# Splitting key loads, reading a flag later and moving a scaling to GpSimd in a four-layer attention kernel

## The reference, cut to what matters

```
x = x + tanh(g_xattn[l]) * cross_attention_l(layernorm(x), ctx, mask_l)
x = x + tanh(g_ffn[l])   * feed_forward_l(layernorm(x))
```

```
attn = softmax(q @ k.T * scale + mask);  out = attn @ v
```

```
topk_scores, idx = top_k(scores, 32);  w = softmax(topk_scores);  out = w @ v[idx]
```

```
l2norm(t) = t / maximum(norm(t), 1e-12)
q = l2norm(q) * q_scale;  k = l2norm(k) * k_scale
q, k = rotary(q), rotary(k)         # local attention over windows of 32
```

## Time and profile before

| what | value |
|---|---|
| median of 3 runs | 8553.93 us (8548.58 to 8557.4) |
| the profiled execution, its own time | 8551.03 us |
| its span in the trace | 8549.2 us |
| mean granted TensorE clock | 0.816 of full |
| VectorE busy | 6960.8 us (81%) |
| TensorE busy | 5875.3 us (69%) |
| ScalarE busy | 4913.9 us (57%) |
| GpSimd busy | 669.4 us (8%) |

### The profile page before, as it was taken

One profiled execution on the slowest core, in us unless ns is written; L12 is line 12 of the kernel. 1 busy time (PEld: TensorE's weight loads), 2 busy tenths in 40 slices (PEclk: granted clock), 3 DMA queues, 4 the chain that ended last, 5 costly groups with the idle time before them and its releaser, 6 DMA issues. The chain is left out here.

```text
span 8549.2 us, 101651 instructions
## 1 busy us (share of the span) xinstructions
PE 5875.3 (69%) x35301; PEld 1769.4 (21%) x35301; DVE 6960.8 (81%) x14058; ACT 4913.9 (57%) x5921; POOL 669.4 (8%) x345
## 2 busy tenths in 40 slices
PE   5588887478888444533554777767788774788887
PEld 1011112111111111100110111144444441111113
DVE  5899991599995699999997999966766675999953
ACT  3177775057778344433444999944444550577782
POOL 1000000000000000000000000043433440000000
PEclk8599998689999555555556999978888885899998
DMA  7100001300000100000002000000000002000001
GB/s 217 28 2 16 16 1 36 77 3 15 16 2 1 24 8 8 8 8 8 8 4 47 16 16 3 1 28 13 13 9 13 11 4 55 3 15 16 2 1 45
DMA packets 111753, 174.94 MB, mean 20 GB/s; under 512 B 14665, under 2 KB 94357, under 8 KB 106254
## 3 DMA queue, kind: packets, MB, share of 16 engines
q1 hardware_dynamic: 111278, 168.91, 7.8%
HBM read 125.66 MB, written 43.21 MB: 20 GB/s over the span
## 5 line engine op out<-in xcount | busy, mean ns | idle before, releaser
L1008 DVE TENSOR_REDUCE a_partial<-a_row 128x1 f32<-128x494 f32 x4992 | 3021.5, 664 | 215.1 <-PE a_row L888 146.2
L974 ACT ACTIVATE a_prob<-a_score 128x1024 f32<-128x1024 f32 x2448 | 2360.5, 1021 | 606.5 <-PE a_score L901 606.2
L888 PE MATMUL a_row<-a_kg,a_qn 54*128 54x494 bf16 x4992 | 1027.8, 409 | 762.7 <-DVE a_partial L1008 660.9
L516 ACT COPY m_rows<-m_score 128x1536 f32<-128x1536 f32 (+1 forms) x640 | 760.9, 1250 | 919.3 <-PE m_score L495 804.1
L913 PE MATMUL a_acc<-a_prob,a_v_all 128*9 128x512 f32 x9792 | 1282.5, 596 | 1.7 <-ACT a_prob L974 1.4
L573 DVE MAX8 m_cand<-m_rows 128x8 f32<-128x192 f32 x4352 | 1220.7, 343 | 13.6 <-ACT m_rows L516 13.2
L495 PE MATMUL m_score<-m_kb,m_qb 54*128 54x512 bf16 (+1 forms) x1664 | 765.9, 608 | 309.4 <-ACT m_rows L516 243.8
L782 DVE SCALAR_TENSOR_TENSOR a_prob<-a_score,a_prob 128x1024 f32<-128x1024 f32 x816 | 924.6, 1211 | 50.3 <-ACT a_prob L758 50.3
L758 ACT ACTIVATE a_prob<-a_score,a_lower 128x1024 f32<-128x1024 f32 x816 | 865.4, 1110 | 72.9 <-PE a_score L701 21.2
L901 PE MATMUL a_score<-a_qb,a_kg 54*128 54x512 bf16 x4896 | 761.1, 379 | 34.7 <-ACT a_prob L974 20.8
L888 PEld LDWEIGHTS a_row<-a_kg,a_qn 54*128 54x128 bf16 x4992 | 241.9, 94 | 2357.4 <-DVE a_partial L1008 2232.4
(11 more groups left out here) (305 smaller groups left out, 5859.1 us busy)
## 6 DMA issues: line engine op xcount, KB each, us to landing
a_kg<-kst SPq DMA_DIRECT2D x64, 306.0 KB
kst<-kv_parts SPq DMA_DIRECT2D x48, 384.0 KB, 3.9
a_v_all<-vst SPq DMA_DIRECT2D x4, 3672.0 KB, 40.7
vst<-kv_va SPq DMA_DIRECT2D x48, 288.0 KB, 4.1
a_kg<-kst SPq DMA_DIRECT2D x64, 204.0 KB
e_cb<-comb SPq DMA_DIRECT2D x25, 512.0 KB
a_kg<-kst SPq DMA_DIRECT2D x64, 102.0 KB
qst<-q_parts SPq DMA_DIRECT2D x24, 256.0 KB, 3.2
```

The source lines that it names most:

```text
L516: act.copy(rows[i][:, c * CH:c * CH + n], score[(i * NCH + c) % 2][:, 0:n]).then_inc(copied, 1)
L888: pe.matmul(row[(use + half) % 3][:, 0:CW], qn[u % 2][rows, pair, i * P:(i + 1) * P], kg[u // NQC % 2][rows, pair, c * CW:(c + 1) * CW], s ...
L974: act.activation(prob[tile % PROBS][:, pair, :, :], score[use % 2][:, :, :], ACT.Exp).then_inc(slot_out, 1)
L1008: dve.tensor_reduce(partial[:, u % 2, 2 * item + half, c:c + 1], row[use % 3][:, 0:CW], AX, ALU.max).then_inc(reduced, 1)
```

## The change

Three edits, in four functions.

1. Key loads. In `attend_with_max` the semaphore of a group's keys becomes two, one for heads 0 and 1 and one for heads 2 and 3; TensorE waits for the first before fill 0 of a unit and for the second before fill 104. In `attend_to_top` the first group's keys are loaded in two column ranges, 768 columns (6 tiles) of all four heads first, then 6 tiles of the values, then the other 5760 columns and the other 45 tiles of the values; TensorE waits for the first parts at tile 0 and for the others at tile 6. That stage has 16 more key transfers and one more of the values.
2. `row_threshold`. `decide` is cut in two. `read_flags` (wait for the count, L552's copy) runs after tile 1 of the next, odd unit, and the rest (register, branch, columns kept, buffers freed) after its tile 8.
3. `local_transformer`. GpSimd scales the keys too, so every step has one `add_halves` and one `scale`. VectorE writes the reciprocal beside a constant 1e12 (a new tile `bounded`, set once by GpSimd) and takes the smaller of the two with a TENSOR_REDUCE.

```diff
-def load_key_rows(sp, dst, kst_h, kmask_l, sem):
+def load_key_rows(sp, dst, kst_h, kmask_l, sem, columns=slice(0, KPAD)):
...
-                     kst_h.rearrange("(d s) c -> d s c", s=PARTS)[:, 0:n, :]).then_inc(sem, 16)
+                     kst_h.rearrange("(d s) c -> d s c", s=PARTS)[:, 0:n, columns]).then_inc(sem, 16)
...
# row_threshold
+    READ_AT, DECIDE_AT = 1, 8
...
-            def decide(pair, slot):
-
+            def read_flags(pair):
                 dve.wait_ge(counted, pair + 2)
                 dve.tensor_copy(taken[:, :], flags[:, :]).then_inc(decided, 1)
+
+            def decide(pair, slot):
+
                 dve.wait_ge(decided, pair + 1)
...
                     last = dve.max(cand[i % 2][:, s, :], rows[i % 4][:, s * W:(s + 1) * W])
+                    if unit >= 3 and unit % 2 and s == READ_AT:
+                        read_flags((unit - 3) // 2)
+                    if unit >= 3 and unit % 2 and s == DECIDE_AT:
+                        decide((unit - 3) // 2, (unit - 3) % 4)
...
-                if i % 2 == 0 and pair is not None:
-                    decide(pair, (i - 2) % 4)
...
# attend_to_top
+    FIRST = 6
...
-            load_keys(0)
-            sp.dma_start(v_all[:, :, :, :], vst_l).then_inc(v_loaded, 16)
+            load_keys(0, kg_first, slice(0, FIRST * P))
+            sp.dma_start(v_all[:, 0:FIRST, :, :], vst_l[:, 0:FIRST, :, :]).then_inc(v_first, 16)
+            load_keys(0, kg_loaded[0], slice(FIRST * P, KPAD))
+            sp.dma_start(v_all[:, FIRST:KT, :, :], vst_l[:, FIRST:KT, :, :]).then_inc(v_loaded, 16)
...
+                    if u:
+                        pe.wait_ge(kg_loaded[u // NQC % 2], G * KEY_LOADS * (u // NQC // 2 + 1))
+                    else:
+                        pe.wait_ge(kg_first, G * KEY_LOADS)
+                if n == 2 * FIRST:
+                    pe.wait_ge(kg_loaded[0], G * KEY_LOADS)
...
                 if tile == 0:
+                    pe.wait_ge(v_first, 16)
+                if tile == FIRST:
                     pe.wait_ge(v_loaded, 16)
...
# attend_with_max
-                        pe.wait_ge(kg_loaded[u // NQC % 2], G * KEY_LOADS * (u // NQC // 2 + 1))
+                        pe.wait_ge(kg_loaded[u // NQC % 2][0], 2 * KEY_LOADS * (u // NQC // 2 + 1))
+                    if n % FILLS == FILLS // 2:
+                        u = n // FILLS
+                        pe.wait_ge(kg_loaded[u // NQC % 2][1], 2 * KEY_LOADS * (u // NQC // 2 + 1))
...
# local_transformer
+            pool.memset(bounded[:, :, :, :], 1.0 / NORM_FLOOR).then_inc(S["cleared"], 1)
...
-            def scale_queries(n):
-                pool.wait_ge(S["rn_q"], n // 2 + 1)
+            def scale(n):
+                pool.wait_ge(S["rn_ready"], n + 1)
...
-                    if s and (s - 1) % 2 == 0:
-                        scale_queries(n - 1)
+                    if s:
+                        scale(n - 1)
...
-            def invert(n, which):
+            def invert(n):
                 dve.wait_ge(S["root"], n + 1)
                 if n >= 2:
-                    dve.wait_ge(S[("scaled_q", "scaled_k")[which]], n // 2)
-                dve.reciprocal(rnorm[:, n % 2, :, :], norm[:, n % 2, :, :]).then_inc(S["inverted"], 1)
+                    dve.wait_ge(S["scaled"], n - 1)
+                dve.reciprocal(bounded[:, n % 2, :, 0:1], norm[:, n % 2, :, :]).then_inc(S["inverted"], 1)
                 dve.wait_ge(S["inverted"], n + 1)
-                if which == 0:
-                    dve.tensor_scalar(rnorm[:, 0, :, :], rnorm[:, 0, :, :], 1.0 / NORM_FLOOR, None,
-                                      ALU.min).then_inc(S["rn_q"], 1)
-                else:
-                    dve.wait_ge(S["added"], n + 1)
-                    dve.scalar_tensor_tensor(out=t1[n % T1S][:, :, :],
-                                             in0=rnorm[:, n % 2, :, :].to_broadcast([P, LH, LD]),
-                                             scalar=1.0 / NORM_FLOOR, in1=t1[n % T1S][:, :, :], op0=ALU.min,
-                                             op1=ALU.mult).then_inc(S["scaled_k"], 1)
+                dve.tensor_reduce(rnorm[:, n % 2, :, 0], bounded[:, n % 2, :, :], AX, ALU.min).then_inc(S["rn_ready"], 1)
```

More of the change, by code:

```diff
@@ L136, in load_key_rows @@
         sp.dma_start(dst[row:row + n * HD, :],
-                     kst_h.rearrange("(d s) c -> d s c", s=PARTS)[:, 0:n, :]).then_inc(sem, 16)
+                     kst_h.rearrange("(d s) c -> d s c", s=PARTS)[:, 0:n, columns]).then_inc(sem, 16)
         row += n * HD
-    sp.dma_start(dst[AUX:ROWS, :], kmask_l).then_inc(sem, 16)
+    sp.dma_start(dst[AUX:ROWS, :], kmask_l[:, columns]).then_inc(sem, 16)
 KEY_LOADS = 16 * (len(PRODUCTS) + 1)
@@ L591, in _ @@
             raise_flag(UNITS - 1, 3, UNITS // 2 - 1)
+            read_flags(UNITS // 2 - 1)
             decide(UNITS // 2 - 1, 2)
@@ L658, in attend_to_top @@
         kg_loaded, qb_loaded = ([m.sem(f"{n}_loaded{i}") for i in range(2)] for n in ("kg", "qb"))
-        cleared, v_loaded = m.sem("cleared"), m.sem("v_loaded")
+        cleared, kg_first, v_first, v_loaded = m.sem("cleared"), m.sem("kg_first"), m.sem("v_first"), m.sem("v_loaded")
         scored, exped, kept, summed = m.sem("scored"), m.sem("exped"), m.sem("kept"), m.sem("summed")
@@ L666, in _, with load_keys @@
         def _(sp):
-            def load_keys(g):
+            def load_keys(g, loaded, columns=slice(0, KPAD)):
                 for j in range(G):
-                    load_key_rows(sp, kg[g % 2][64 * (j % 2):64 * (j % 2) + ROWS, j // 2, :], kst_l[g * G + j], kmask_l,
-                                  kg_loaded[g % 2])
+                    load_key_rows(sp, kg[g % 2][64 * (j % 2):64 * (j % 2) + ROWS, j // 2, columns], kst_l[g * G + j], kmask_l,
+                                  loaded, columns)
             def load_queries(u):
@@ L678, in _ @@
             load_queries(0)
-            load_keys(0)
-            sp.dma_start(v_all[:, :, :, :], vst_l).then_inc(v_loaded, 16)
+            load_keys(0, kg_first, slice(0, FIRST * P))
+            sp.dma_start(v_all[:, 0:FIRST, :, :], vst_l[:, 0:FIRST, :, :]).then_inc(v_first, 16)
+            load_keys(0, kg_loaded[0], slice(FIRST * P, KPAD))
+            sp.dma_start(v_all[:, FIRST:KT, :, :], vst_l[:, FIRST:KT, :, :]).then_inc(v_loaded, 16)
             load_queries(1)
-            load_keys(1)
+            load_keys(1, kg_loaded[1])
             for u in range(UNITS - 2):
@@ L686, in _ @@
                 if u % NQC == 1 and u // NQC + 2 < NG:
-                    load_keys(u // NQC + 2)
+                    load_keys(u // NQC + 2, kg_loaded[u // NQC % 2])
         @block.tensor
@@ L816, in attend_with_max @@
         row = [m.ps(f"row{i}", [P, QC]) for i in range(3)]
-        kg_loaded, qn_loaded = ([m.sem(f"{n}_loaded{i}") for i in range(2)] for n in ("kg", "qn"))
+        qn_loaded = [m.sem(f"qn_loaded{i}") for i in range(2)]
+        kg_loaded = [[m.sem(f"kg_loaded{i}{pair}") for pair in range(2)] for i in range(2)]
         cleared, v_loaded = m.sem("cleared"), m.sem("v_loaded")
@@ L849, in load_keys @@
                     load_key_rows(sp, kg[g % 2][64 * (j % 2):64 * (j % 2) + ROWS, j // 2, :], kst_l[g * G + j], kmask_l,
-                                  kg_loaded[g % 2])
+                                  kg_loaded[g % 2][j // 2])
             def load_queries(u):
@@ L1564, in local_transformer @@
         norm, rnorm = m.sb("norm", [P, 2, LH, 1]), m.sb("rnorm", [P, 2, LH, 1])
+        bounded = m.sb("bounded", [P, 2, LH, 2])
         ssq = m.sb("ssq", [P, 2, LH])
@@ L1573, in local_transformer @@
             "cleared", "setup", "loaded", "wqk", "wvo", "w12", "tables", "shifted",
-            "proj", "squared", "roped", "added", "summed_sq", "root", "inverted", "rn_q", "scaled_q", "scaled_k", "turned_qk", "kept_qk",
+            "proj", "squared", "roped", "added", "summed_sq", "root", "inverted", "rn_ready", "scaled", "turned_qk", "kept_qk",
             "v_done", "v_kept", "sc_done", "maxed", "exped", "rs_ready", "rinv_ready", "normed", "turned", "pt_ready",
@@ L1627, in turn_heads @@
                 n = layer * STEPS + s
-                pe.wait_ge(S[("scaled_q", "scaled_k")[s % 2]], n // 2 + 1)
+                pe.wait_ge(S["scaled"], n + 1)
                 if s:
@@ L1934, in keep @@
                                     S["o_ready"], 1)
-            dve.wait_ge(S["cleared"], 3)
+            dve.wait_ge(S["cleared"], 4)
             dve.wait_ge(S["loaded"], 16 * 7)
@@ L1948, in _ @@
                     if s:
-                        invert(n - 1, (s - 1) % 2)
+                        invert(n - 1)
                 for t in range(LT + 2):
```

3 lines of the change are left out of this document (1 added, 2 removed).

## The result

The changed kernel takes 8318.35 us (median of 4 runs, 8317.42 to 8321.43), the kernel before 8552.7 us (4 runs, 8548.58 to 8557.4): ratio 0.9726, 95% interval 0.971 to 0.9743. That is 234.4 us faster. The spans of the two profiled executions, 8549.2 and 8315.6 us, differ by 233.6 us, and that can be split by stage, from the same event in both timelines to the next.

The account below looks back on a forecast made before the run. VectorE was taken to set the pace in layer 2's search and the local transformer, with key waits at stage starts. 46 + 8 + 60 + 81 - 0.6 = 194 us off 8551.0 gave 8360 us on the median's basis, range 8325 to 8432.

Parts of the forecast that it names:

- Keys by head pair: Three stages with a maximum: first fill comes 15.5 us earlier in each, 46 us in all (ends 12 and 52).
- a further head costs 8.1 us: Key loads: each head beyond the first adds 8.1 us from issue to fill, so two heads take 18.7 us.
- Rival C: Key loads: first pair's keys share bandwidth with transfers queued behind, 12 us gained instead of 46, time 8394; chance 0.07.
- Keys by columns: Layer 2's attention to the top: sums of tile 6 start earlier, 8 us gained (ends -4 and 14); values late next.
- Flags: Layer 2's search: decision hidden behind VectorE's queued work, 0.95 us in each of 63, 60 us (ends 0 and 66).
- rival A: Search: register load and branch drain VectorE's queue, decision stays in the open, 60 us less gained, 8420; chance 0.17.
- GpSimd: Local transformer: scaling keys on GpSimd shortens the step from 5.31 us, 81 us in six layers (ends 39 and 93).
- 4.35 a step with gaps: Local transformer's first phase: GpSimd's addition and scaling, 4.24 us of work, set a step of 4.35 us including gaps.
- before and behind them the path is as now: Local transformer: only the 14 steps between first and last scaling gain; the rest of each layer gains nothing.
- The reduce: Local transformer: the 128 x 16 reduce replacing VectorE's bounding instructions takes 0.25 us, making VectorE's step 3.97 us.
- Rival B: Local transformer: TensorE at 1.2 GHz sets the step, 5.31 us or more, that edit gives 0, 8441; chance 0.10.
- Rival D: Local transformer: VectorE and GpSimd exclude each other throughout, step 8.2 us, slower at 8683; chance 0.03.

Follow-up runs that it names:

- pairs alone: The kernel before with only the waits by head pair added in the three stages with a maximum: 8506.18 us (10 runs), ratio 0.9952.

## Why the prediction was right, and where it was not

Two terms of the sum failed, both too small: 60 us for the flags, where 76.6 were measured, and 81 us for the scaling, where it was 100.9. Together that is 36.5 us; the terms of the keys were right to 3 us each.

- **Keys by head pair**: right, 43.5 for 46. The working with "a further head costs 8.1 us" gave 18.7 us for two heads; they took 17.3, 18.3 and 19.2, and 16.6 to 19.8 in all kernels with these waits and whole rows. So 2 us of such a term are the transfers' own spread. Layer 3's wait was shorter before (32.02 us) and gave only 11.4. Rival C (12 us) is out: pairs alone give 44.2.
- **Keys by columns**: right, 11.2 for 8: keys and values landed 2 to 3 us earlier than worked out (+37.9 and +51.6). The sums of tile 6 moved by 11.9 us and the stage by 11.2, so starting again cost 0.7 us and not 1.5. The wait behind the gain is the one named.
- **Flags**: the mechanism was right, the term "0.95 us hidden in each of 63" was mis-sized, and so was its end, "66 (63 times 1.05)". I took the 1.05 us of one piece in the earlier trace rows for all, although the row that groups them, has 71.1 us in 63 pieces, 1.13 each: 13 of them are of 1.35 us and more, so that "the same in nearly all" under rival A was wrong too. And idle time is not the whole price: operations that follow each other overlap by some 0.07 us in the records, and a stop takes that away too. 76.6/63 is 1.22 us. I then took a tenth off for a cover that held fully. Rival A (8420) is out.
- **GpSimd**: the mechanism was right, and it is GpSimd that is late next. The term "4.35 a step with gaps" was mis-sized: the steps are 4.18 us, and 14 of them take 59.24 us in the first layer, which has a slower one, and 58.5 to 58.6 in the other five, 4.19 each on the mean, where 14 took 74.34. That gives 94.1 us in six layers for 81. Its end, 4.2 a step, was passed by a hair, and it bounded the 14 steps only. The other 6.8 us were not in the sum: "before and behind them the path is as now" failed by 1.1 us a layer. Little of that lies at the phase's own edges (15.8 us less from the first addition to the first scores, 15.7 of them in the 14 steps); about 1 us lies behind it, where TensorE is back at its upper level one group sooner. That this clock is the cause is argued, not shown.
- **The reduce**: 0.19 for 0.25, VectorE's step 3.85 for 3.97. Rival B is out: TensorE idles 1.37 us before a turn, not under a microsecond as I had written, and even so has a granted clock of 0.96. Rival D is out too (L1910 takes 1.23 us beside GpSimd, 1.21 before).
- **The range**: its low end was set just below 8329, the sum of four upper ends, of which two were too low: 66 against the 71 of its own row and 76.6 measured, and 93 for the 14 steps of a layer, against 94.1 measured for these and 100.9 for the stage. I treated them as ends that can't be passed, though they carried the errors of the terms themselves.

## What to carry to other kernels

Size a stall from the row that counts all its pieces, never from one of them, and add the overlap that a stop takes away. Before a decision in a full engine, put queued work between the last operation whose end it waits for and the decision, not only between the data and its use. When a stage's start waits for a transfer, let it wait for the bytes of its first few steps: the wait shrank with the bytes each time. The first part has to last until the rest is there, though: with 6 of 51 tiles TensorE was through in 15 us and then waited 13.7, with 16 it never waited.

## What I had not expected of the hardware

- A wait, register load and branch on VectorE cost 1.05 us of idle time in most pairs and up to 1.76 with an empty queue, and nothing visible with work queued, in every pair but the last. The load has the largest share, 0.30 us, and the branch instruction itself 0.06.
- GpSimd's operations follow each other without a gap: 2.39 + 1.93 us of work recorded in a step of 4.18 us.
- The time from issue to use went roughly with the bytes: 31.6 to 34.9 us for four heads, 17.3 to 19.2 for two, and 6.7 to 7.0 for 45% of the columns of two. Where 12% of four heads' columns went first, the 16 issues took 7.9 of the 9.2 us.
- A VectorE operation of 16 elements a partition can take 1.15 us beside GpSimd's addition and 1.82 beside its scaling, ending 0.03 us after it each time, and another form of the same work 0.19.
